# First-pass attention scores issued in twos, one per half of the TensorE array

## The chip, the cores and the metric

The kernel runs on one core of one Trainium2 chip. The metric is the time of one execution on the device in microseconds (us). Three runs of the kernel before gave 1682.65, 1682.81 and 1683.82 us; the median is 1682.81 us.

## The reference

Two blocks follow each other on x of shape (4, 1024, 128), all in float32. Both have 16 heads of width 8.

```python
# block 1
x = x + ln(attn_alibi_causal(ln(x)))     # scores*scale + alibi bias, causal mask, softmax, @v, @Wo
# block 2, on ln(x)
h = h + ln(attention(h)) * g1 + b1       # no mask: every query sees all 1024 keys
h = h + ln(moe(h)) * g2 + b2             # top 2 of 8 experts, gelu(h@W1[e])@W2[e]
x = x + ln(h)
```

Softmax needs the maximum of each row of scores (or a value that plays its part). The kernel finds it in a pass of its own.

## The kernel before, in words

Each attention layer is cut into 16 **slots**: a batch (4) times a group of four heads. Slots 0 to 15 are the causal layer, 16 to 31 the layer without a mask; `SLOTS` is 32. In a slot every head is computed twice.

- **First pass, "a"** (lines 374 to 395): scores with the queries on the 128 partitions of PSUM and up to 512 keys along them; VectorE takes the maximum of each row (`tensor_reduce`, line 589). A head's operands take 32 rows, and one matmul has 64 rows of the array as its contraction (`PAIR`): heads 0 and 1 use the upper half of the array, heads 2 and 3 the lower. Such a matmul is a **chunk**: (query tile, key half, heads, keys). A causal slot has 40 chunks, the other kind 64. They are listed in the head order 0, 2, 1, 3, so neighbours 2k and 2k+1 have the same shape and lie on different halves of the array. When a causal chunk meets the diagonal, two bf16 matmuls (line 393) add the mask into its last 128 keys; 24 of 40 chunks do.
- **Turn, "m" and "mtr"**: when all chunks of a slot are reduced, VectorE combines the maxima (lines 598 to 603), TensorE transposes them (line 399), VectorE copies them out (line 609), and they go into the operands as more rows, so that the second pass yields score minus maximum.
- **Second pass, "b"** (line 411): scores with the keys on the partitions, 512 queries or fewer; ScalarE takes the exponential (line 474) into `probs`. **"pv"** (line 424) multiplies by the values: 4 heads side by side in columns of the array, 8 matmul instructions. Finished outputs are evicted by ScalarE (line 479, "oev").

The work is written out by hand as one list of steps (`program`, lines 174 to 217). Slot s is a loop over its `nq` key tiles (12 when causal, 16 otherwise), called step i here. Step i issues, in this order: the first "b" of tile i+3, half of the step's chunks, the second "b", the other chunks, the third and fourth "b", perhaps "m" or "mtr", then "pv" of tile i+1, and row work such as projections ("turn", "q", "k", "project"). The chunks of a step belong to a later slot: in the first `a_steps` steps to slot s+1 (16 chunks over 5 steps when that is causal, 36 over 9 otherwise), in the last seven to slot s+2 (24 or 28 chunks). They are spread evenly, so that a step has three or four chunks in the causal layer; in the other it has four, except that the turn's step (`mt_step`, the first of the last seven, i = 5 or 9) has three and the step three later has five.

What orders the engines: each engine walks the same list in order and waits on counting semaphores. PSUM has a ring of four banks (`A_BANKS`) for chunks, the turn's transpose and all row matmuls; `bank_free` lets a step have a bank only when the step four places earlier in the ring was read. "b" has three banks, so a "b" waits for the exponential three before it. `probs` has four buffers.

Of the kernel before, what the change touches and what calls it, by code (L numbers as in the profile page):

```python
# [26 lines left out]
P = 128  # L27
# [13 lines left out]
HALF = 512  # L41
# [16 lines left out]
LOADS = 16 * 3 * GH  # L58
# [4 lines left out]
PAIR = 2 * HW  # L63
# [45 lines left out]
def plan_of(s):  # L109
    return PLANS[s // S]  # L110


def place_of(s):

    return s // S, s % S // G, s % G
# [57 lines left out]
def program():  # L173


    rows = row_steps()
    first, second = plan_of(0), plan_of(1)
    out = [("a", 0, c) for c in range(first.na)] + [("m", 0, 0), ("mtr", 0, 0)]
    bs = [("b", 0, i) for i in range(GH * LEAD)]
    ass = [("a", 1, c) for c in range(second.a_next)]  # L180
    for i in range(GH):
        out += ass[len(ass) * i // GH:len(ass) * (i + 1) // GH] + bs[i:i + 1]
    out += [("stage", 0, 0)] + bs[GH:] + [("pv", 0, 0)]
    for s in range(SLOTS):
        p = plan_of(s)
        if s + 3 < SLOTS:
            out.append(("load", s + 3, 0))
        if s + 1 < SLOTS:
            out.append(("stage", s + 1, 0))
        weights = [4 - (i == p.mt_step) - .5 * (i == p.m_step) for i in range(p.nq)]  # L190
        for i in range(p.nq):
            early = i < p.a_steps
            part = range(p.a_steps) if early else range(p.a_steps, p.nq)
            target = s + 1 if early else s + 2
            ass = []
            if target < SLOTS:
                t = plan_of(target)
                base, n = (t.a_next, t.na - t.a_next) if early else (0, t.a_next)
                total = sum(weights[k] for k in part)
                lo = int(n * sum(weights[k] for k in part if k < i) / total + .5)  # L200
                hi = int(n * sum(weights[k] for k in part if k <= i) / total + .5)
                ass = [("a", target, base + c) for c in range(lo, hi)]
            q = i + LEAD
            at, q = (s, q) if q < p.nq else (s + 1, q - p.nq)
            bs = [("b", at, q * GH + j) for j in range(GH)] if at < SLOTS else []
            half = (len(ass) + 1) // 2
            out += bs[:1] + ass[:half] + bs[1:2] + ass[half:] + bs[2:]
            if s + 1 < SLOTS:
                if i == p.m_step:
                    out.append(("m", s + 1, 0))  # L210
                if i == p.mt_step:
                    out.append(("mtr", s + 1, 0))
            at, q = (s, i + 1) if i + 1 < p.nq else (s + 1, 0)
            if at < SLOTS:
                out.append(("pv", at, q))
                if q in plan_of(at).half_end:
                    out.append(("oev", at, plan_of(at).half_end.index(q)))
            out += rows.get((s, i), [])
    return out
# [18 lines left out]
def attend(nc, loaded, query, key, rests, tokens, sums, by_head, dens, inverses, inverse_rows, ident, half_ident,  # L238
           half_mask, km, fq, x_rows, kept_u, wo, bo, wv, bv, wqk, bqk, rows, gate_w, gate_b, gw, tri, rank, table, pows, W1,
           W2, w_parts, routing, xs):  # L240
    steps = program()
    with ExitStack() as ctx:
        def sb(name, shape, dt=F32):
            return ctx.enter_context(nc.sbuf_tensor(f"at_{name}", shape, dt))

        def sem(name):
            return ctx.enter_context(nc.semaphore(f"at_{name}"))
# [26 lines left out]
        raw, parts = sb("raw", [P, FF]), sb("parts", [P, 2, FF], F32R)  # L274

        a_made, a_read = sem("a_made"), sem("a_read")
# [32 lines left out]
        def done(eng, semaphore, kind, s, n, per=1):  # L309

            if (s, n) in number.get(kind, {}):
                eng.wait_ge(semaphore, per * number[kind][s, n])

        def after(eng, name, key):

            r = (name,) + key
            if r in row_number:
                eng.wait_ge(row_done[ENGINE_OF[name]], row_number[r])
# [11 lines left out]
        def query_columns(s, t):  # L330
            qh, kt = plan_of(s).quads[t]
            q0 = max(qh * HALF, kt * P) if plan_of(s).causal else qh * HALF
            return qh, kt, q0, (qh + 1) * HALF - q0

        def bank_of(step):
            return a_bank[place[step] % A_BANKS]
# [13 lines left out]
        def layer(stage):  # L350
            return 0 if stage == "first" else 1
# [4 lines left out]
        def _(pe):  # L356
            def bank_free(step):

                if place[step] < A_BANKS:
                    return  # L360
                what, s, n = ring[place[step] - A_BANKS]
                if what == "a":
                    done(pe, a_read, "a", s, n)
                elif what == "mtr":
                    done(pe, m_read, "mtr", s, n)
                else:
                    reader = dict(project="y", turn="turned", values_mm="values", q="q_out", k="k_out", logits="gate",
                                  rank="pos")[what]
                    after(pe, reader, n)

            for step in steps:
                what, s, n = step
                if what in RING:
                    bank_free(step)
                    misc = bank_of(step)
                if what == "a":
                    l, b, g = place_of(s)
                    qt, kh, heads, w = plan_of(s).chunks[n]

                    if n == 0:  # L380
                        pe.wait_ge(loaded, LOADS * (s + 1))
                    diagonal = plan_of(s).causal and kh * HALF + w == (qt + 1) * P

                    k = len(heads)
                    scores = misc[:, 0:k * w].rearrange("p (k w) -> p k w", k=k)
                    rows_ = slice(PAIR * (heads[0] // 2), PAIR * (heads[0] // 2 + 1))
                    first = heads[0] % 2
                    mm = pe.matmul(scores, fq[g][rows_, qt * P:(qt + 1) * P],  # L388
                                   km[g][rows_, first:first + k, kh * HALF:kh * HALF + w],
                                   start=True, stop=not diagonal)  # L390
                    if diagonal:
                        for i in range(2):
                            mm = pe.matmul(scores[:, :, w - P:w], half_ident[rows_, i, :],  # L393
                                           half_mask[rows_, i, None, :].broadcast_to([PAIR, k, P]),
                                           start=False, stop=(i == 1))
                    mm.then_inc(a_made, 1)
                elif what == "mtr":
                    done(pe, m_split, "m", s, 0)
                    pe.transpose(misc[:, 0:P], m_parts[:, :, :, :].rearrange("p j k t -> p (j k t)").bitcast(F32),
                                 ident[:, :]).then_inc(m_turned, 1)  # L400
                elif what == "b":
                    l, b, g = place_of(s)
                    t, j = n // GH, B_HEADS[n % GH]
                    qh, kt, q0, w = query_columns(s, t)
                    if n == 0:
                        pe.wait_ge(m_landed, MAX_ROWS * (s + 1))
                    k = number["b"][s, n] - 1
                    if k >= B_BANKS:
                        pe.wait_ge(exp_done, k + 1 - B_BANKS)
                    rows_ = slice(PAIR * (j // 2), PAIR * (j // 2 + 1))  # L410
                    pe.matmul(b_bank[k % B_BANKS][:, 0:w], km[g][rows_, j % 2, kt * P:(kt + 1) * P],  # L411
                              fq[g][rows_, q0:q0 + w], start=True, stop=True).then_inc(b_made, 1)
                elif what == "pv":
                    p = plan_of(s)
                    qh, kt, q0, w = query_columns(s, n)
# [7 lines left out]
                    for j in range(GH):  # L423
                        mm = pe.matmul(pv_bank[HW * j:HW * (j + 1), HALF - w:HALF], vst[s % 2][:, kt, j, :],  # L424
                                       probs[n % PROBS][:, j, 0:w], start=(kt == 0), stop=(n == p.half_end[qh]))
                    mm.then_inc(pv_done, 1)
                elif what in ROW_ENGINE["pe"]:
                    stage, k = n
                    i = layer(stage)
                    if what == "project":  # L430
                        after(pe, "heads_t", n)
                        for t in range(HQ):
                            mm = pe.matmul(misc[:, t * P:(t + 1) * P], heads_t[:, t * P:(t + 1) * P],
                                           wo[1 if stage == "enter" else 0][:, :], start=True, stop=True)
                    elif what == "turn":
                        after(pe, "w" if stage == "enter" else "norm2b", n)
                        src = normed[:, :, :] if stage == "first" else block_of(kept_u, k)
                        for t in range(HQ):
                            mm = pe.transpose(misc[:, t * P:(t + 1) * P], src[:, t, :], ident[:, :])
                    elif what == "values_mm":  # L440
                        after(pe, "turned", n)
                        for t in range(HQ):
                            mm = pe.matmul(misc[:, t * P:(t + 1) * P], t32[:, t * P:(t + 1) * P], wv[i][:, :],
                                           start=True, stop=True)
                    elif what in ("q", "k"):
                        after(pe, "low", n)
                        m = "qk".index(what)
                        mm = three(pe, misc[:, :], [part[:, m, :] for part in wqk[i]], [part[:, :] for part in turned])
                    elif what == "logits":
                        after(pe, "low", n)  # L450
                        pe.wait_ge(gw_made, 2)
                        for t in range(HQ):
                            mm = three(pe, misc[:, t * E:(t + 1) * E], [m[:, t * P:(t + 1) * P] for m in turned],
                                       [m[:, :] for m in gw])
                    elif what == "rank":
                        after(pe, "seen", n)
                        pe.matmul(misc[:, 0:TB * E], tri[:, 0, :], routing["either"][:, :, :].rearrange("p t e -> p (t e)"),
                                  start=True, stop=False)
                        mm = pe.matmul(misc[:, 0:TB * E], tri[:, 1, :],
                                       routing["seen"][:, pair_of(k), :].rearrange("p t e -> p (t e)"),  # L460
                                       start=False, stop=True)
# [1419 lines left out]
```

## Time and profile before

| what | value |
|---|---|
| median of three runs | 1682.81 us |
| the profiled execution | 1682.8 us |
| its span, first to last instruction | 1681.1 us |
| TensorE busy | 1424.7 us, 85% |
| VectorE busy | 1296.1 us, 77% |
| ScalarE busy | 1097.2 us, 65% |
| mean granted TensorE clock | 0.915 |

Busy time of TensorE counts matmuls in flight; their ends are modelled, and matmuls on the two halves of the array overlap, so a busy share near one does not say that the array is full. Attention lasts from about 113 us to 1346 us; what follows is the expert layer.

### The profile page before, as it was taken

How to read it: one execution, taken by the hardware profiler on the slowest of the kernel's cores; microseconds unless marked ns; L12 is line 12 of the kernel's file. 1: busy time of each engine (PE TensorE's matmuls, PEld its weight loads, DVE VectorE, ACT ScalarE, POOL GpSimd, SP SyncE). 2: the span in 40 equal slices, each digit the busy share in tenths (PEclk: the TensorE clock that was granted, in tenths of full speed). 3: DMA queues.
4: the chain of work that ended last, by engine and by line, in shares of the span. 5: the costliest groups of instructions: out<-in, count | busy, mean ns of one | idle time of the engine just before them, and what ended most of it. 6: DMA issues, size and time to landing. Idle time of an engine off the chain costs nothing. (4 is left out here: it accounts for less than half of the span.)

```text
span 1681.1 us, 27511 instructions
## 1 busy us (share of the span) xinstructions
PE 1424.7 (85%) x9143; PEld 712.0 (42%) x9143; DVE 1296.1 (77%) x2638; ACT 1097.2 (65%) x2256; POOL 536.7 (32%) x624
## 2 busy tenths in 40 slices
PE   3389999999999999999999999999999831999400
PEld 3145555555555443443344333433343221788300
DVE  4378888889888989999999999999998023655355
ACT  4036677677676557778777787778777820999444
POOL 5114544534525322340122312323141406000274
PEclk9569999999999989999999999999999965999855
DMA  6402241322322222133221122102210124788322
GB/s 168 145 28 73 84 133 50 112 81 65 102 89 72 74 71 66 43 90 91 69 65 53 52 64 78 54 32 75 61 46 33 57 78 131 224 247 248 110 63 69
DMA packets 105822, 148.96 MB, mean 89 GB/s; under 512 B 13236, under 2 KB 63164, under 8 KB 105680
## 3 DMA queue, kind: packets, MB, share of 16 engines
q1 hardware_dynamic: 100348, 138.18, 28.0%
q0 software_dynamic: 4096, 8.40, 1.7%
q8 instruction: 73, 1.20, 0.3%
q10 hardware_dynamic: 1236, 0.62, 0.2%
q14 instruction: 69, 0.57, 0.1%
HBM read 78.70 MB, written 67.13 MB: 87 GB/s over the span
## 5 line engine op out<-in xcount | busy, mean ns | idle before, releaser
L474 ACT ACTIVATE at_probs<-at_b 128x512 f32<-128x512 f32 (+3 forms) x1792 | 866.3, 557 | 380.8 <-PE at_b L411 376.2
L589 DVE TENSOR_REDUCE at_mx<-at_a 128x1 f32<-128x512 f32 (+3 forms) x1664 | 992.0, 661 | 89.5 <-PE at_a L393 28.3
L411 PE MATMUL at_b<-fq,km 64*128 64x512 f32 (+3 forms) x1792 | 669.1, 439 | 16.7 <-ACT at_probs L474 13.3
L388 PE MATMUL at_a<-km,fq 64*128 64x512 f32 (+2 forms) x1664 | 549.9, 453 | 46.3 <-DMA fq<-rest 35.2
L411 PEld LDWEIGHTS at_b<-fq,km 64*128 64x128 f32 x1792 | 295.9, 187 | 405.0 <-ACT at_probs L474 340.5
L424 PE MATMUL at_pv<-at_probs,at_vst 128*32 128x512 f32 (+3 forms) x3584 | 442.0, 566 | 0.0
L388 PEld LDWEIGHTS at_a<-km,fq 64*128 64x128 f32 x1664 | 273.8, 191 | 146.2 <-DVE at_mx L589 82.9
L747 POOL TENSOR_SCALAR_AFFINE_SELECT at_probs<-at_probs 128x512 f32<-128x512 f32 x128 | 81.5, 636 | 284.0 <-ACT at_probs L474 283.1
L1653 POOL DMA_INDIRECT t_got<-expert_out,t_out_pos x64 | 63.5, 993 | 171.4 <-issue 171.4
L424 PEld LDWEIGHTS at_pv<-at_probs,at_vst 128*32 128x32 f32 x3584 | 71.0, 108 | 104.2 <-issue 49.2
L393 PE MATMUL at_a<-half_mask,half_ident 64*128 64x128 bf16 (+1 forms) x768 | 108.7, 251 | 0.0
L1566 DVE TENSOR_TENSOR t_hid_lo<-t_hid,t_hid_hi 128x512 fp32r<-128x512 f32 x92 | 61.3, 686 | 60.5 <-ACT t_hid_hi L1419 60.5
L1414 ACT ACTIVATE t_hid<-t_bank_h,t_bias 128x512 f32<-128x512 f32 x92 | 63.0, 687 | 2.7 <-PE t_bank_h L235 2.6
L752 POOL DMA_INDIRECT expert_rows<-kept_u,route_pos x48 | 46.7, 974 | 36.5 <-DVE route_pos L873 23.5
L1419 ACT ACTIVATE t_hid_hi<-t_hid 128x512 fp32r<-128x512 f32 x92 | 55.5, 635 | 0.0
L393 PEld LDWEIGHTS at_a<-half_mask,half_ident 64*128 64x128 bf16 x768 | 43.2, 100 | 25.6 <-issue 17.4
L1577 DVE SCALAR_TENSOR_TENSOR t_z<-t_got,route_weight,t_weighed 128x128 f32<-128x128 f32 x32 | 9.1, 346 | 47.4 <-ACT t_weighed L1428 47.4
L637 POOL TENSOR_TENSOR at_rstd<-at_mean_var,pow_cols 128x4 f32<-128x4 f32 x26 | 5.3, 203 | 124.9 <-DVE at_mean_var L501 124.9
L479 ACT ACTIVATE at_osb<-at_pv 128x512 f32<-128x512 f32 x64 | 39.4, 615 | 6.2 <-PE at_pv L424 1.9
L741 POOL COPY at_vst<-tokens 128x256 f32<-128x256 f32 x32 | 12.7, 397 | 95.3 <-PE at_pv L424 95.0
L637 POOL TENSOR_TENSOR at_turned_hi<-at_t,pow_cols 128x512 fp32r<-128x512 f32 x18 | 18.7, 1041 | 69.4 <-DVE at_t L532 69.4
L233 PE MATMUL t_bank_h<-t_x_t_hi,t_w 128*128 128x512 f32 x92 | 37.0, 402 | 3.1 <-issue 1.6
(237 smaller groups left out, 1254.2 us busy)
## 6 DMA issues: line engine op xcount, KB each, us to landing
t_w<-w_parts SPq DMA_DIRECT2D x46, 512.0 KB, 4.4
sums<-at_osb SPq DMA_DIRECT2D x64, 256.0 KB, 2.0
fq<-query SPq DMA_DIRECT2D x128, 96.0 KB
km<-key SPq DMA_DIRECT2D x128, 96.0 KB
w_parts<-at_parts SPq DMA_DIRECT2D x16, 512.0 KB, 3.0
query<-at_q_hi SPq DMA_DIRECT2D x24, 256.0 KB, 3.1
key<-at_k_hi SPq DMA_DIRECT2D x24, 256.0 KB, 3.7
t_x_tok<-expert_rows SPq DMA_DIRECT2D x23, 256.0 KB, 4.8
```

The lines of the kernel that those rows point to most:

```text
L388: mm = pe.matmul(scores, fq[g][rows_, qt * P:(qt + 1) * P], km[g][rows_, first:first + k, kh * HALF:kh * HALF + w], start=True, stop=not d ...
L393: mm = pe.matmul(scores[:, :, w - P:w], half_ident[rows_, i, :], half_mask[rows_, i, None, :].broadcast_to([PAIR, k, P]), start=False, sto ...
L411: pe.matmul(b_bank[k % B_BANKS][:, 0:w], km[g][rows_, j % 2, kt * P:(kt + 1) * P], fq[g][rows_, q0:q0 + w], start=True, stop=True).then_in ...
L424: mm = pe.matmul(pv_bank[HW * j:HW * (j + 1), HALF - w:HALF], vst[s % 2][:, kt, j, :], probs[n % PROBS][:, j, 0:w], start=(kt == 0), stop= ...
L474: act.activation(probs[t % PROBS][:, j, 0:w], b_bank[k % B_BANKS][:, 0:w], ACT.Exp).then_inc(exp_done, 1)
L589: dve.tensor_reduce(mx[:, kh, qt, heads[0]:heads[0] + k], bank_of(step)[:, 0:k * w].rearrange("p (k w) -> p k w", k=k), AX.X, ALU.max).the ...
L747: pool.affine_select(block_, block_, [[0, GH], [1, P]], ALU.is_ge, 0.0, base=0, channel_multiplier=-1).then_inc(masked, 1)
L752: pool.indirect_dma_start(out=xs[:, :], out_offset=bass.IndirectOffsetOnAxis(ap=routing["pos"][:, k, t:t + 1], axis=0), in_=kept_u[:, t, : ...
L1414: op = act.activation(hid[:, f, :], h_bank[f][:, :], ACT.Gelu, bias=bias[:, n, f:f + 1])
L1419: op = act.activation(hid_hi[i][:, f, :], hid[:, f, :], ACT.Identity)
L1566: op = dve.tensor_tensor(hid_lo[i][:, f, :], hid[:, f, :], hid_hi[i][:, f, :].bitcast(F32), ALU.subtract)
L1653: pool.indirect_dma_start(out=got[i][:, k, t, :], out_offset=None, in_=ys[:, :], in_offset=bass.IndirectOffsetOnAxis(ap=out_pos[:, k, n * ...
```

## The change

Three things change, in `program` and in TensorE's walk.

1. The boundaries of the chunks of a step are rounded to even numbers, and so is the place where the step's chunks are split around its second "b". Every step has 2, 4, 6 or 8 chunks, always whole pairs.
2. TensorE takes a pair at a time: the bank and the score of the first chunk, the bank and the score of the second, then mask matmul 1 of both, then mask matmul 2 of both (before: score, mask 1, mask 2 of one chunk, then the same of the next).
3. Nothing changes for the other engines but the order of the list.

```diff
-                lo = int(n * sum(weights[k] for k in part if k < i) / total + .5)
-                hi = int(n * sum(weights[k] for k in part if k <= i) / total + .5)
+                lo = 2 * int(n * sum(weights[k] for k in part if k < i) / total / 2 + .5)
+                hi = 2 * int(n * sum(weights[k] for k in part if k <= i) / total / 2 + .5)
...
-            half = (len(ass) + 1) // 2
+            half = 2 * ((len(ass) + 2) // 4)
...
+            def first_scores(pair):
+                parts = []
+                for step in pair:
+                    what, s, n = step
+                    bank_free(step)
+                    l, b, g = place_of(s)
+                    if n == 0:
+                        pe.wait_ge(loaded, LOADS * (s + 1))
+                    qt, kh, heads, w = plan_of(s).chunks[n]
...
+                    mm = pe.matmul(scores, fq[g][rows_, qt * P:(qt + 1) * P],
+                                   km[g][rows_, heads[0] % 2:heads[0] % 2 + k, kh * HALF:kh * HALF + w],
+                                   start=True, stop=not diagonal)
+                    if diagonal:
+                        parts.append((rows_, k, scores[:, :, w - P:w]))
+                    else:
+                        mm.then_inc(a_made, 1)
+                for i in range(2):
+                    for rows_, k, corner in parts:
+                        mm = pe.matmul(corner, half_ident[rows_, i, :],
+                                       half_mask[rows_, i, None, :].broadcast_to([PAIR, k, P]),
+                                       start=False, stop=(i == 1))
+                        if i == 1:
+                            mm.then_inc(a_made, 1)
+
+            for at_, step in enumerate(steps):
                 what, s, n = step
+                if what == "a":
+                    if n % 2 == 0:
+                        assert steps[at_ + 1] == ("a", s, n + 1)
+                        first_scores(steps[at_:at_ + 2])
+                    continue
```

By the formula, a causal slot's steps i = 0 to 11 had 3, 4, 3, 3, 3, 3, 3, 4, 3, 4, 3, 4 chunks and get 4, 2, 4, 4, 2, 2, 4, 4, 4, 2, 4, 4. In a slot of the second layer steps 9 to 15 had 3, 4, 4, 5, 4, 4, 4 and get four each; steps 0 to 8 have four before and after.

## Rows read from the trace of the kernel before

**Rows 1.** Stretches: start:end, PE, PEld, DVE, ACT, POOL busy us, clock, DMA share, GB/s
```profile
113.00:571.80 458.80, 453.66 (x3678) 235.12 (x3677) 398.73 (x829) 320.68 (x750) 205.85 (x261) 1.00 0.28 84
619.90:1314.40 694.50, 676.40 (x4036) 275.26 (x4035) 636.93 (x1167) 516.98 (x995) 177.35 (x199) 0.99 0.21 63
571.80:619.90 48.10, 45.85 (x228) 20.32 (x227) 43.43 (x80) 23.02 (x51) 14.66 (x18) 0.86 0.11 30
```
**Rows 2.** Waits of the weight loads: us in total, times, longest us
```profile
PEld at_b L411 <- ACT at_probs L474: 340.5, 552, 1.7
PEld at_a L388 <- DVE at_mx L589: 82.9, 295, 1.9
```
**Rows 3.** Timeline (start us, us, engine, operation), a step of slot 24
```profile
1002.38 0.50 PE L411 MATMUL at_b<-fq,km 64*128 64x512 f32 x1
...
1002.91 2.06 ACT L474 ACTIVATE at_probs<-at_b 128x512 f32<-128x512 f32 x4 [0.54 <-PE at_b L411]
...
1003.56 0.18 PEld L411 LDWEIGHTS at_b<-fq,km 64*128 64x128 f32 x1 [0.29 <-ACT at_probs L474]
...
1004.98 0.50 PE L411 MATMUL at_b<-fq,km 64*128 64x512 f32 x1
```
**Rows 4.** Timeline, ScalarE, slot 31, whose steps have no chunks
```profile
1323.74 2.07 ACT L474 ACTIVATE at_probs<-at_b 128x512 f32<-128x512 f32 x4 [0.53 <-PE at_b L411]
1326.34 2.07 ACT L474 ACTIVATE at_probs<-at_b 128x512 f32<-128x512 f32 x4 [0.53 <-PE at_b L411]
```
**Rows 5.** Timeline, TensorE, slot 8, step 8, chunks 10 to 12
```profile
380.15 0.33 PE L411 MATMUL at_b<-fq,km 64*128 64x128 f32 x1
380.16 0.59 PE L388 MATMUL at_a<-km,fq 64*128 64x512 f32 x2
380.51 0.28 PE L393 MATMUL at_a<-half_mask,half_ident 64*128 64x128 bf16 x2
380.60 0.30 PE L411 MATMUL at_b<-fq,km 64*128 64x128 f32 x1
380.61 0.28 PE L393 MATMUL at_a<-half_mask,half_ident 64*128 64x128 bf16 x2
...
381.16 0.53 PE L424 MATMUL at_pv<-at_probs,at_vst 128*32 128x384 f32 x4
```
**Rows 6.** Timeline, VectorE, reduces of slot 8's steps 7 and 8 from chunk 6
```profile
378.66 3.55 DVE L589 TENSOR_REDUCE at_mx<-at_a 128x1 f32<-128x384 f32 x6 [0.71 <-PE at_a L393]
```
**Rows 7.** Timeline, slots 8 and 9: reduces from chunk 20, then step 0 on TensorE
```profile
359.25 4.38 DVE L589 TENSOR_REDUCE at_mx<-at_a 128x1 f32<-128x512 f32 x7 [0.16 <-PE at_a L388]
...
361.10 0.33 PE L411 MATMUL at_b<-fq,km 64*128 64x128 f32 x1
...
362.05 0.53 PE L424 MATMUL at_pv<-at_probs,at_vst 128*32 128x384 f32 x4
```
**Rows 8.** Timeline, TensorE, step 9 of slot 8: four chunks
```profile
381.94 0.50 PE L411 MATMUL at_b<-fq,km 64*128 64x512 f32 x1
...
383.24 0.48 PE L411 MATMUL at_b<-fq,km 64*128 64x512 f32 x1
```
**Rows 9.** Timeline, the turn's step of slot 19
```profile
787.13 0.50 PE L411 MATMUL at_b<-fq,km 64*128 64x512 f32 x1
...
788.39 1.87 DVE L589 TENSOR_REDUCE at_mx<-at_a 128x1 f32<-128x512 f32 x3
788.73 0.14 PEld L399 LDWEIGHTS at_a<-ident,at_m_parts 128*128 128x128 f32 x1 [0.24 <-issue]
```
**Rows 10.** Stretches that are steps 8, 9 (turn), 10 and 12 (five chunks) of slot 21
```profile
877.95:880.56 2.61, 2.61 (x17) 1.01 (x16) 2.50 (x5) 2.06 (x4) 0.00 (x0) 1.00 0.00 0
880.57:883.43 2.86, 2.86 (x20) 1.15 (x16) 2.72 (x14) 2.06 (x4) 0.06 (x1) 1.00 0.00 0
883.44:886.76 3.32, 3.12 (x20) 1.18 (x16) 3.32 (x7) 2.08 (x4) 2.60 (x4) 1.00 0.01 2
...
889.38:892.34 2.96, 2.66 (x21) 1.10 (x17) 2.86 (x5) 2.17 (x4) 1.05 (x1) 1.00 0.00 0
```
**Rows 11.** Timeline, the turn's step of slot 21
```profile
882.18 0.14 PEld L399 LDWEIGHTS at_a<-ident,at_m_parts 128*128 128x128 f32 x1 [0.25 <-issue]
...
883.01 1.85 DVE L589 TENSOR_REDUCE at_mx<-at_a 128x1 f32<-128x512 f32 x3
```
**Rows 12.** Slot 20's turn: TensorE, and the stretch behind it
```profile
833.42 0.45 PE L399 MATMUL at_a<-ident,at_m_parts 128*128 128x128 f32 x1 [1.81 <-DVE at_m_parts L603]
833.80 1.93 PE L424 MATMUL at_pv<-at_probs,at_vst 128*32 128x512 f32 x8
...
837.57 1.06 PE L424 MATMUL at_pv<-at_probs,at_vst 128*32 128x512 f32 x8
```

More of the change, by code:

```diff
@@ L369, in bank_free @@
                     after(pe, reader, n)
-            for step in steps:
-                what, s, n = step
+            def first_scores(pair):
[7 more added lines that the diff above has]
+                    qt, kh, heads, w = plan_of(s).chunks[n]
+                    k = len(heads)
+                    scores = bank_of(step)[:, 0:k * w].rearrange("p (k w) -> p k w", k=k)
+                    rows_ = slice(PAIR * (heads[0] // 2), PAIR * (heads[0] // 2 + 1))
+                    diagonal = plan_of(s).causal and kh * HALF + w == (qt + 1) * P
+                    mm = pe.matmul(scores, fq[g][rows_, qt * P:(qt + 1) * P],
[13 more added lines that the diff above has]
+            for at_, step in enumerate(steps):
+                what, s, n = step
+                if what == "a":
[3 more added lines that the diff above has]
+                    continue
                 if what in RING:
@@ L375, in _ @@
                     misc = bank_of(step)
[L376 to L397, printed above, removed]
+                if what == "mtr":
                     done(pe, m_split, "m", s, 0)
```

## The prediction

> **What bounds the kernel now.** I read four views, in this order. The table by stretch comes first [rows 1]: the causal layer (113 to 572 us) and the unmasked one (620 to 1314 us) make up two thirds of the span. In both TensorE is busy 97 to 99% by the profile and VectorE 87 to 92%. Two engines near full can't both be the bound, so the rest is reading which wait ends last in a step.
>
> The waits say it [rows 2]: the second pass's weight loads wait 340.5 us for ScalarE's exponentials, the first pass's 82.9 us for VectorE's reduces. The timeline of a plain step shows how [rows 3]. A "b" starts at 1002.38, its exponential at 1002.91 (0.53 later) and takes about 0.6; then the step's fourth "b" may load its weights, at 1003.56; "pv" comes 0.43 behind, and the next first "b" at 1004.98. That loop, "b", exponential, fourth "b", "pv", is 2.60 us long. The proof that chunks hide in it is slot 31, which has none: its exponentials also come 1326.34 - 1323.74 = 2.60 us apart [rows 4]. So a step costs the loop, and a chunk costs something only where it makes the third or fourth "b", the turn or "pv" later than the loop would. In the causal layer the loop is shorter where "b" or "pv" is narrow, so there the cover is thinner.
>
> **The change part by part.**
>
> *Mask order.* It removes no instruction: 768 mask matmuls before and after. What it could gain is overlap of the halves. The diagonal step shows that the halves already run past each other [rows 5]: the list says b, score, mask, mask, score, mask, mask, b, and yet both scores start before the first mask (380.16, two in 0.59 us), and the second "b" (380.60) starts before the last two masks (380.61). A half's own sequence is the same before and after, so I take 0. The upper end of a gain is that the second score of a diagonal pair lost one score and two masks, about 0.23 + 0.13 us by the starts in these rows; the lower end is a loss where the second chunk's bank comes late, since the masks of the first now stand behind that wait: one reduce, 0.6 us, but then VectorE has older chunks to work on. Value 0.
>
> Here the Trainium skill differs. "TensorE: Matmul & The Clock Gate", section "Part 3: Packing small matmuls", says that matmuls start and end strictly in program order and only weight loads are pulled ahead. By that rule the old order would have held the second score behind the first one's masks, and the new order would free it; the trace does not agree, since the starts just read cross program order. What the rule would make of the time is the first rival below.
>
> *Causal layer, uneven steps.* Two steps that had three narrow-loop chunks get four.
> - Step 0. The new fourth chunk needs the bank of chunk 23. Seven reduces start at 359.25, about 0.6 us apart [rows 7]; the fourth, chunk 23's, ends near 361.73, which is 0.63 after step 0's first "b" (361.10). Then load and score, 0.1 + 0.23, the fourth "b" and "pv": about 1.17 after the first "b", where "pv" stood at 0.95 (362.05). Cost 0.22. In 12 of 15 slots; in three a projection stands ahead and the bank is free. 2.6 us.
> - Step 8. The new chunk 13 needs chunk 9's bank. Six reduces from 378.66 last 3.55 in all [rows 6], so the fourth (chunk 9) ends near 380.9, 0.73 after the first "b". By the same sum "pv" comes 1.26 after it instead of 1.01 (381.16 - 380.15) [rows 5]. Cost 0.25, in the 11 slots without row work right there: 2.8 us.
> - Steps 9 and 1 had four chunks and get two. The last "b" stood 1.30 behind the first (383.24 - 381.94) [rows 8], against 1.18 in the loop [rows 3]. A gain of 0.09 and 0.05, in 15 slots: -2.1 us.
> - A norm's statistics stall step 2 in six slots by some 0.4 us; fewer chunks queue behind them: about -0.1 each, -0.6 us (an estimate from the reduce's 0.6 us spacing).
> Sum +2.7 us. Its ends: -3, if the fourth chunks cost nothing and the stalls go, and +8, if each costs one reduce more.
>
> *Unmasked layer, the turn's step.* It gets a fourth chunk, and that moves the ring. The transpose used to take the bank of the previous step's last chunk, long read. Now it takes the bank of this step's first chunk, whose reduce stands behind VectorE's chain for the turn. In a quiet slot that reduce starts at 788.39 and ends 0.68 later, 789.07, while the transpose loaded its weights at 788.73 [rows 9]: 0.38 late, and "pv" with it. In slot 21 VectorE does a norm's statistics between: the reduces start at 883.01, the first ends near 883.67, the transpose stood at 882.18 [rows 11]: 1.5 late. There are three such slots (21, 25, 29; by the same reading 1.5 to 1.8).
>
> *The step of five.* It goes: 2.96 against 2.61 us [rows 10], -0.36. In slot 21 step 10 was also stretched, 3.32 against 2.61 [rows 10], since its chunks waited for the late reduces; when "pv" is 1.5 later this wait lies beside it: -0.7.
>
> By kind of slot: three like 21 cost 1.5 (1.8 once) - 0.7 (1.0 once) - 0.36, so +0.43 each, +1.3. Quiet ones +0.38 - 0.36 = 0 (four). Four with a projection, as slot 20: there the chain for the turn ended at 833.2 and the first reduce behind it ends at 833.9, so +0.5; their five-chunk step with a projection loses 0.5; 0. In slots 22 and 26 VectorE works without a pause through these steps, so the count of reduces decides and that is the same: 0. Slots 14, 15 and 17 shift a reduce into a step with room, -0.6 in all. Sum +0.7.
>
> *The clock.* In slot 20 TensorE stood idle 1.81 us before the transpose, and "pv" then took 1.93 us instead of 1.06: the granted clock was at the lower of its levels (1.2 GHz) behind it. From "pv" to "pv" took 3.77 instead of 2.60 us [rows 12], so a fall costs 1.2 us. It follows such an idle in four of four slots. The three slots like 21 will now stand idle some 1.7 to 2 us. I count one and a half falls, +1.8; ends 0 and 3 x 1.2 = 3.6 (and 4 x 1.2 more if the falls of the four project slots get a second stretch).
>
> **Sum.** 2.7 + 0.7 + 1.8 = +5.2 us on the profiled execution's 1682.8 us (span 1681.1 and 1.7 around it), which is the median of the runs shown. Forecast 1688.0 us.
>
> **Rivals.**
> *A, matmuls in program order.* Then the mask order gains. For: the profile models the ends of matmuls. Against: the starts of [rows 5]. It would decide only where a half's queue sets "pv": two diagonal steps of a causal slot (7 and 8; elsewhere the exponential is later), some 0.25 us of the 0.36 each, in 16 slots: -8. Time 1680. (The rule of the skill named above is this one.) Chance 0.12.
> *B, the stalls and slow-clock stretches at the layers' seam go.* Slots 14 and 15 have to make 28 + 36 chunks of the wide kind; in 571.8 to 619.9 us VectorE is busy 43.4 of 48.1 us and the granted clock is 0.86 [rows 1]. If whole pairs keep TensorE fed so that four slow stretches there and one in slot 22 don't occur, 5 x 1.2 = 6 us come off, and about 2 more if the turn's step is less delayed: 1688 - 8 = 1680. It decides when TensorE's idle between reduces shortens. Against: that stretch is set by VectorE's reduces, whose number is the same. On the other side of no change. Chance 0.15.
> *C, the fourth chunks cost nothing.* If a chunk overlaps with its half's "b" more than I allow, the causal sum is about 0 and falls of the clock stay one: 1684.5. Chance 0.18.
> *D, more falls.* All seven lengthened idles bring a slow stretch, 7 x 1.2 in place of 1.8, and the steps at the seam with eight chunks add to it: 1695. Chance 0.1.
>
> **How the numbers follow.** The forecast has the rest, 0.45, its own range 1685.5 to 1691. A measurement tells 0.2%, 3.4 us, from no change: 1679.4 and 1686.2. Faster gets half of A and two thirds of B, 0.16. Same gets the other parts of A and B (0.11), most of C (0.16) and 0.04 of the forecast, 0.31. Slower is what is left, 0.53. The range 1679 to 1696 takes in A, B and D; the bounds of the causal sum (-3 to +8) lie within it.
>
> **What the changed profile would show.** The turn's transpose (line 399) with waits for VectorE in nearly all slots from 16 on, up to 1.5 us in slots 21, 25 and 29; no step of 2.96 us, steps of four chunks at 2.60 unchanged; causal steps 0 and 8 longer by 0.2 us, 1 and 9 shorter by less than 0.1; mask matmuls with the same starts relative to their half; a clock below 1.00 near slots 21, 25 and 29. I am wrong if the transpose starts as early as before, if diagonal steps get shorter by 0.2 us, or if the seam (slots 14 and 15) changes by more than 2 us.

## The result, and the profile after

The change made the kernel slower: 1697.41 us (median of 4 runs, 1693.94 to 1697.74) against 1683.32 us (4 runs, 1682.65 to 1684.06). The ratio is 1.0084, 95% interval [1.0071, 1.0097], so some 14 us where 5 had been forecast. The profiled execution took 1697.7 us (span 1696.0); in it TensorE was busy 1429.0 us, VectorE 1297.7 and ScalarE 1097.1, as before within 0.3%, at a mean granted clock of 0.912. The work is the same; the waits are not. Below are the stretches of the kernel after (columns as in [rows 1]): the causal slots 0 to 14, the seam (slot 15), and slots 16 to 31.

```profile
112.48:581.55 469.07, 459.97 (x3678) 234.88 (x3677) 399.27 (x829) 323.23 (x750) 205.83 (x261) 0.99 0.28 82
581.55:632.20 50.65, 48.41 (x229) 21.39 (x228) 43.61 (x79) 23.25 (x51) 14.65 (x18) 0.76 0.10 28
632.20:1365.14 732.94, 702.77 (x4208) 281.82 (x4211) 638.03 (x1167) 542.81 (x1049) 192.94 (x215) 0.99 0.21 63
```
[Rows 1] has the causal slots and the seam of the kernel before, 458.8 and 48.1 us; its unmasked row stops earlier, so here is the whole of slots 16 to 31 of the kernel before:

```profile
619.92:1350.05 730.13, 706.05 (x4208) 284.04 (x4211) 636.91 (x1167) 545.31 (x1049) 193.21 (x215) 0.99 0.21 63
```
So +10.2 us in the causal slots, +2.6 at the seam, +2.8 in the unmasked layer. The causal part is the surprise. The waits of the weight loads (columns as in [rows 2]) both grew: behind ScalarE from 340.5 us and 552 times, behind VectorE from 82.9 us and 295 times.

```profile
PEld at_b L424 <- ACT at_probs L487: 357.4, 599, 1.6
PEld at_a L385 <- DVE at_mx L602: 90.9, 350, 1.9
```
To see where, take the distance from the start of one "pv" to the start of the next as the length of a step. Slot 8 has no row matmul; its slot time went from 27.39 to 28.12 us, as in slots 4 and 12. The step lengths in us, for both kernels and for two experiments told below (chunks in brackets where they differ):

| step | before | after | fours_0_8 | fours_6_10 |
|---|---|---|---|---|
| 11 of slot 7 | 1.86 | 2.24 | 1.86 | 2.22 |
| 0 | 1.94 (3) | 2.09 (4) | 2.17 (4) | 1.94 (3) |
| 1 | 2.42 (4) | 2.40 (2) | 2.40 (3) | 2.39 (3) |
| 6 | 2.38 (3) | 2.38 (4) | 2.38 (3) | 2.38 (4) |
| 7 | 2.21 | 2.56 | 2.21 | 2.56 |
| 8 | 2.01 (3) | 2.01 (4) | 2.27 (4) | 2.00 (3) |
| 9 | 2.48 (4) | 2.39 (2) | 2.39 (3) | 2.39 (3) |
| 10 | 2.00 (3) | 1.96 (4) | 1.96 (3) | 1.95 (4) |

The loss is in steps 7 and 11, which have four chunks in every column. Step 7 of the kernel before, TensorE from its first "b" to "pv", then VectorE:

```profile
377.94 0.38 PE L411 MATMUL at_b<-fq,km 64*128 64x256 f32 x1
...
378.44 0.49 PE L388 MATMUL at_a<-km,fq 64*128 64x512 f32 x2
378.76 0.29 PE L393 MATMUL at_a<-half_mask,half_ident 64*128 64x128 bf16 x4
378.85 0.37 PE L411 MATMUL at_b<-fq,km 64*128 64x256 f32 x2
379.15 0.64 PE L424 MATMUL at_pv<-at_probs,at_vst 128*32 128x512 f32 x4
...
376.33 1.62 DVE L589 TENSOR_REDUCE at_mx<-at_a 128x2 f32<-128x512 f32 x3 [0.75 <-PE at_a L393]
378.66 1.02 DVE L589 TENSOR_REDUCE at_mx<-at_a 128x1 f32<-128x384 f32 x2 [0.71 <-PE at_a L393]
```
The same step of the kernel after, TensorE with its weight loads, then VectorE:

```profile
384.49 0.38 PE L424 MATMUL at_b<-fq,km 64*128 64x256 f32 x1
...
385.32 0.18 PEld L385 LDWEIGHTS at_a<-km,fq 64*128 64x128 f32 x1 [0.17 <-DVE at_mx L602]
...
385.42 0.36 PE L424 MATMUL at_b<-fq,km 64*128 64x256 f32 x1
385.67 0.28 PE L394 MATMUL at_a<-half_mask,half_ident 64*128 64x128 bf16 x2
385.76 0.36 PE L424 MATMUL at_b<-fq,km 64*128 64x256 f32 x1
386.05 0.64 PE L437 MATMUL at_pv<-at_probs,at_vst 128*32 128x512 f32 x4
...
383.05 3.78 DVE L602 TENSOR_REDUCE at_mx<-at_a 128x2 f32<-128x512 f32 x7 [1.55 <-PE at_a L394]
```
Before, step 6 leaves three reduces. They end at 376.33 + 1.62 = 377.95, just as step 7 starts, and VectorE then stands idle 0.71 us: each bank that step 7 wants is free. After, step 6 leaves four; VectorE works on without a pause, and the fourth reduce (chunk 5's) ends near 383.05 + 4 x 0.54 = 385.2, 0.7 after the step's first "b" (384.49). The ring has four banks, so the fourth chunk of step 7 (chunk 9) takes chunk 5's: it loads at 385.32, released by VectorE. Its masks and the last "b" stand behind it. That "b" comes 1.27 after the first, where before the last two "b" came 0.91 after the first, and "pv" with it: +0.35. Step 11 does the same behind step 10 (chunk 23 takes chunk 19's bank), with two such waits in the rows of the kernel after:

```profile
393.26 0.18 PEld L385 LDWEIGHTS at_a<-km,fq 64*128 64x128 f32 x1 [0.20 <-DVE at_mx L602]
393.86 0.18 PEld L385 LDWEIGHTS at_a<-km,fq 64*128 64x128 f32 x1 [0.41 <-DVE at_mx L602]
...
392.20 3.40 DVE L602 TENSOR_REDUCE at_mx<-at_a 128x2 f32<-128x256 f32 x6
```
The second kind of loss is in steps with a row matmul and a new fourth chunk. In slots 1 to 3 the step with "q" went from 2.90 to 3.29 us. A row matmul takes a ring bank too, and the step's new fourth chunk is four places behind it. In the row of slot 1 after, that chunk waits for VectorE to evict "q", and two "b" wait with it, where in before the same two "b" loaded 0.63 after the step's first one:

```profile
170.03 0.18 PEld L424 LDWEIGHTS at_b<-fq,km 64*128 64x128 f32 x1 [0.36 <-issue]
...
170.95 0.18 PEld L385 LDWEIGHTS at_a<-km,fq 64*128 64x128 f32 x1 [0.20 <-DVE at_q_out L557]
170.95 0.29 PEld L424 LDWEIGHTS at_b<-fq,km 64*128 64x128 f32 x2
```
The step with "project" in slots 5, 9 and 13 went from 3.06 to 3.42 in the same way: in slot 5 the fourth chunk waits 0.45 us for VectorE to evict the projection. The step with the values' matmul in slots 0 to 3 went from 3.47 to 3.66, and in slots 7 and 11 two steps with a row matmul grew by 0.40 and 0.25; what holds these is not shown. There are gains too: the stall behind the norm's statistics fell from 2.57 to 2.43 in slots 1 to 3 and to 2.27 in slots 5, 9 and 13, step 9 by 0.09 in most slots, and step 1 by 0.2 to 0.3 in slots 6, 7, 10, 11 and 14.

A part of the causal loss is the clock's. Step 1 of slot 0, of the kernel before and of the kernel after:

```profile
116.33:118.73 2.40, 2.40 (x24) 1.28 (x23) 2.37 (x9) 1.53 (x5) 0.64 (x1) 1.00 0.00 0
115.83:119.17 3.34, 3.34 (x20) 1.69 (x19) 3.31 (x13) 1.50 (x4) 0.63 (x1) 0.61 0.00 0
```
The +0.95 stands beside a clock of 0.61 in place of 1.00. Two of the experiments told below agree: the same step takes 3.34 at a clock of 0.67 in short_before, which has the old numbers of chunks, and 2.54 in even_only, which has the new ones.

Added up over slots 0 to 14, steps 7 and 11 cost 7.3 us, the steps with a row matmul 4.7, step 0 elsewhere 1.9 and this stretch 0.95; all other steps together give back 4.6. By slot: +1.6 in slot 0, +2.9 in slots 1 to 3, +2.2 in 4, 8, 12, +0.8 in 5, 9, 13, +1.1 in 6 and 10, +1.7 in 7 and 11, -0.1 in 14; together +10.2.

The seam grew in steps 0 to 4 of slot 15, which have six to eight chunks: from 28.13 us at a mean clock of 0.76 to 30.85 at 0.61. Behind them, at full clock in both kernels, its turn's step went from 2.86 to 3.28 and its former five-chunk step from 2.93 to 2.33.

In the unmasked layer the turn's step of slot 19, then that of slot 21 and its former five-chunk step, of the kernel after:

```profile
798.47:801.71 3.24, 2.93 (x19) 1.15 (x18) 3.14 (x8) 2.70 (x7) 0.00 (x0) 1.00 0.00 0
...
892.91:897.32 4.41, 2.93 (x19) 1.15 (x18) 4.27 (x16) 3.05 (x7) 0.54 (x2) 1.00 0.00 0
902.53:905.14 2.61, 2.61 (x18) 1.01 (x17) 2.49 (x5) 2.07 (x6) 1.21 (x1) 1.00 0.00 1
```
They were 2.86, 2.86 and 2.96 us ([rows 10] for slot 21). The transpose waits for the step's own first chunk, in slot 21 behind VectorE's statistics; rows of slot 19 and of slot 21 after:

```profile
801.45 0.14 PEld L412 LDWEIGHTS at_a<-ident,at_m_parts 128*128 128x128 f32 x1 [0.62 <-DVE at_mx L602]
...
895.15 0.86 DVE L511 BATCH_NORM_STATS2 at_stats<-at_y 128x6 f32<-128x128 f32 x4
...
896.35 1.25 DVE L602 TENSOR_REDUCE at_mx<-at_a 128x1 f32<-128x512 f32 x2
897.06 0.14 PEld L412 LDWEIGHTS at_a<-ident,at_m_parts 128*128 128x128 f32 x1 [1.79 <-DVE at_mx L602]
```

### The profile page after: what moved, and what is told of

It is laid out like the page before. It is cut to its first block and busy times, and to the rows that moved or that the text cites. A ratio compares the mean times of both kernels' runs of the same rounds, so it can differ in the third digit from the quotient of the medians.

```text
span 1696.0 us, 27511 instructions
## 1 busy us (share of the span) xinstructions
PE 1429.0 (84%) x9143; PEld 709.2 (42%) x9143; DVE 1297.7 (77%) x2638; ACT 1097.1 (65%) x2256; POOL 537.4 (32%) x624
## 5 line engine op out<-in xcount | busy, mean ns | idle before, releaser
L424 PE MATMUL at_b<-fq,km 64*128 64x512 f32 (+3 forms) x1792 | 682.9, 438 | 18.4 <-ACT at_probs L487 10.8
L424 PEld LDWEIGHTS at_b<-fq,km 64*128 64x128 f32 x1792 | 304.4, 188 | 418.0 <-ACT at_probs L487 357.4
```

## Experiments

In all of them "slots 0 to 14" is the stretch from the first "pv" of slot 0 to that of slot 15, 458.9 us in the kernel before and 469.1 after.

**even_only: even numbers, old mask order.**

```diff
-                        first_scores(steps[at_:at_ + 2])
+                        first_scores([step])
```


> Even numbers of chunks per step, but each chunk with its own two masks behind it, as before. Theory 1 (VectorE's reduces run late behind steps of four, so the fourth chunk waits for its bank and holds back the last b of the next step): within 2 us of the changed kernel, 1695 to 1699, and causal steps 0, 7 and 11 as long as there (2.22 us for the one that ends at pv 0, 2.55 at pv 8). Rival 2 (the interleaved masks cost the 0.35 us, since both long steps, 7 and 11, are steps with masks): these steps fall back to 1.86 and 2.21, and the time to about 1688.

Measured 1693.66 us, ratio 1.0072 [1.0051, 1.0093]; slots 0 to 14 took 468.5 us. Its step 7 of slot 8:

```profile
382.77:385.32 2.55, 2.55 (x27) 1.33 (x25) 2.55 (x6) 1.76 (x6) 0.63 (x1) 1.00 0.12 35
```
The loss is there without the new mask order, and so is the long step 7. The time came out just under the 1695 to 1699 expected and 3.7 us below the kernel after. That is not the mask order at work on the causal steps: slots 1 to 14 take as long in both within 0.1 us, and the difference lies where the clock was low in one of them, in slot 0 (-0.6), at the seam (49.1 us at a clock of 0.83) and in the unmasked layer (730.3 us).

**masks_only: old numbers, masks of both chunks interleaved where a pair stands together.**

```diff
-                lo = 2 * int(n * sum(weights[k] for k in part if k < i) / total / 2 + .5)
+                lo = int(n * sum(weights[k] for k in part if k < i) / total + .5)
...
+                    if n % 2 == 0 and steps[at_ + 1] == ("a", s, n + 1):
+                        pair, taken = steps[at_:at_ + 2], {at_ + 1}
```


> The numbers of chunks of before; where the two chunks of a pair follow each other in the list, scores first and then the masks in turn. Theory 1: no change, within 1 us of the kernel before (about 1683.3), steps 7 and 11 at 2.21 and 1.86. Rival 2: steps 7 and 11, where both pairs are adjacent, become 0.3 longer, 15 slots x 0.65 = +10 us. A kernel whose matmuls ran in program order would get faster by some us.

Measured 1683.42 us, ratio 1.0003 [0.9993, 1.0013]; slots 0 to 14: 458.7 us, every step of slot 8 as before within 0.01. TensorE in its step 7:

```profile
377.36 0.38 PE L429 MATMUL at_b<-fq,km 64*128 64x256 f32 x1
...
377.86 0.48 PE L386 MATMUL at_a<-km,fq 64*128 64x512 f32 x2
378.18 0.29 PE L395 MATMUL at_a<-half_mask,half_ident 64*128 64x128 bf16 x4
378.27 0.36 PE L429 MATMUL at_b<-fq,km 64*128 64x256 f32 x2
```
The starts after the first "b" (0.50, 0.82, 0.91) are those of before (0.50, 0.82, 0.91). The mask order is worth nothing measurable.

**even_causal and even_plain: the new numbers for the chunks of one layer, new mask order in both.**

```diff
+                unit = 2 if target < S else 1      # even_plain: target >= S
+                lo = unit * int(n * sum(weights[k] for k in part if k < i) / total / unit + .5)
```


> The change for chunks of causal slots only; chunks of slots 16 to 31 keep the old numbers. Theory 1: +10 us over before (slots 0 to 14), slot 15 and the second layer as before: 1693. If the late layer change is what matters: 1684.

> The change for chunks of slots 16 to 31 only. Theory 1: steps of slots 0 to 13 as before, the turn's step 3.25 instead of 2.86 and the step of five 2.60 instead of 2.97 in quiet slots, sum zero; +2.5 in slot 15 and +3 in the second layer with its slow clock stretches: 1686 to 1689.

Measured: even_causal 1692.95 us, 1.0058 [1.004, 1.0076]; even_plain 1686.2 us, 1.0024 [1.0011, 1.0036]. About +10 and +4 us: the two parts add up to the whole, and the larger is the causal layer's. Slots 0 to 14 took 468.8 and 459.4 us. The seam did not follow the expectation: even_causal was to leave it as before, and it took 49.7 us at a clock of 0.73; in even_plain it took 50.4 at 0.76.

**short_before and short_after: VectorE's reduces in the causal layer over half their columns.** Both leave out the other half of each maximum there.

```diff
-                                      bank_of(step)[:, 0:k * w].rearrange("p (k w) -> p k w", k=k),
+                                      bank_of(step)[:, 0:k * w].rearrange("p (k w) -> p k w", k=k)[:, :, 0:w // (2 if s < S else 1)],
```


> The kernel before with one thing left out: in the causal layer (slots 0 to 15) VectorE takes the maximum over the first half of a chunk's columns only, so a reduce lasts about 0.34 instead of 0.60 us. Control for the next run. Theory 1: slots 0 to 14 lose only what little hung on reduces, some 0.3 us in a quiet slot (27.4 to about 27.0) and the stalls behind statistics; slot 15, which is bound by reduces, gets far shorter.

> The same cut of the causal reduces in the changed kernel. Theory 1 (late reduces hold the banks): steps 0, 7 and 11 fall back to the lengths of the control (about 1.94, 2.21 and 1.86), and slots 0 to 14 take as long as in the control within 2 us. Rival (a half of the array has too much in one step of four chunks, whatever VectorE does): the three steps stay 0.16, 0.34 and 0.36 us longer than in the control, +10 us in slots 0 to 14.

Measured 1666.24 and 1673.42 us (ratios to the kernel before 0.9902 [0.9879, 0.9926] and 0.9947 [0.993, 0.9965]). Slots 0 to 14: 452.8 and 456.6. The difference of the two rules fell from 10.2 to 3.9 us. Step 1 of slot 0, with its slow clock, is long in the kernel after (3.34) but here in short_before (3.34 against 2.50 in short_after); without that step the difference fell from 9.3 to 4.7. In slot 8 steps 0, 7 and 11 are 1.94, 2.21 and 1.90 us in short_after, against 1.94, 2.21 and 1.86 in short_before. VectorE in step 7 of short_after:

```profile
366.89 1.28 DVE L602 TENSOR_REDUCE at_mx<-at_a 128x2 f32<-128x256 f32 x4 [1.55 <-PE at_a L394]
369.05 0.95 DVE L602 TENSOR_REDUCE at_mx<-at_a 128x1 f32<-128x192 f32 x3 [0.88 <-PE at_a L394]
```
The same four reduces of step 6 now end at 368.17, before step 7 starts (368.33), and the pause is back. So it is the late reduces that make steps 7 and 11 long, not the number of chunks. What stays is the row work: "q" 3.29 against 2.90, "project" 3.46 against 3.07, the step with the values 3.66 against 3.47. My expectation that slot 15 would get far shorter in short_before missed: it took 49.9 us. The chunks worked on there belong to slots 16 and 17, whose reduces are whole in both kernels.

**turn_later: the kernel after, with the transpose of the unmasked slots one step later.**

```diff
-                if i == p.mt_step:
+                if i == p.mt_step + (s >= S):
```


> The changed kernel with the turn's transpose of slots 17 to 31 issued at the end of the step after (step 10 instead of 9). Its bank is then that of step 10's first chunk. If the wait for the reduce behind VectorE's chain is what made the turn's step 3.25, the two steps together fall from 5.85 to about 5.65 (quiet slot), since the reduces are only 0.6 late by then and the transpose waits 0.2; in slots 21, 25 and 29 from 7.0 to 6.0 and without slow clock stretches. Time 1692, 5 below the changed kernel. If the wait is for something else (the chain itself or a DMA), no change.

Measured 1694.57 us, 1.0071 [1.005, 1.0092] to the kernel before; 1692 had been expected. The two steps concerned in slot 19, and the second of them in slot 21:

```profile
795.62:798.22 2.60, 2.60 (x18) 1.01 (x17) 2.50 (x7) 2.07 (x6) 0.00 (x0) 1.00 0.00 0
798.22:801.32 3.10, 3.00 (x18) 1.07 (x17) 3.10 (x6) 2.43 (x6) 0.00 (x0) 1.00 0.00 0
892.37:896.63 4.26, 4.00 (x18) 1.43 (x18) 4.23 (x13) 2.54 (x6) 2.34 (x4) 1.00 0.00 0
```
In slot 19 3.24 + 2.60 became 2.60 + 3.10, and in slot 21 the delay moved one step on (4.41 to 4.26). My expectation that a later turn would take most of it away there failed: the delay is VectorE's queue, and whoever stands behind it pays.

**fours_0_8 and fours_6_10: the old numbers but for which steps of a causal slot have four chunks.** The list gives chunks of steps 0 to 4 and 5 to 11 (before: 3, 4, 3, 3, 3 and 3, 3, 4, 3, 4, 3, 4).

```diff
+COUNTS = {(True, True, True): (4, 3, 3, 3, 3), (True, True, False): (3, 3, 4, 4, 3, 3, 4)}   # fours_0_8
+COUNTS = {(True, True, True): (3, 3, 4, 4, 2), (True, True, False): (2, 4, 4, 3, 3, 4, 4)}   # fours_6_10
...
+                    lo, hi = sum(own[:at_]), sum(own[:at_ + 1])
```


> The kernel before with four chunks in steps 0 and 8 of a causal slot (early counts 4,3,3,3,3, late 3,3,4,4,3,3,4), so those are the only steps of the causal layer with one more chunk, and steps 7 and 11 find the statistics of three-chunk steps before them. The prediction's own term (fourth chunk costs what its score chain costs): step 0 of a quiet slot 1.94 to 2.16 us, step 8 2.01 to 2.26, slots 0 to 14 +2 to +3 us. Theory of the bank (a fourth chunk pays where the bank that it writes is still being read): steps 7 and 11 stay at 2.21 and 1.86; the q step of slots 0 to 3 goes from 2.90 to 3.29 and the project step of slots 5, 9, 13 from 3.06 to 3.42, because the fourth chunk takes the bank of the row matmul; quiet step 8 gains nothing or under 0.1. Slots 0 to 14: +3 to +4.5 us, median +2 to +4. Rival (the loss sits in the number of chunks per step as such): the same +0.35 in steps 0 and 8 here.

> The kernel before with four chunks in steps 6, 7, 10 and 11 (early counts 3,3,4,4,2, late 2,4,4,3,3,4,4), steps 0 and 8 as before or shorter. Theory of the bank: four chunks in steps 6 and 10 make their statistics end late, and the fourth chunk of steps 7 and 11 waits for the banks: step 7 of a quiet slot 2.21 to 2.55, step 11 1.86 to 2.22; the q step and the project step keep 2.90 and 3.06. Slots 0 to 14: +4 to +6 us, median +4 to +6. The prediction's own term (score chains of steps 0 and 8 alone): steps 7 and 11 unchanged, slots 0 to 14 within 1 us of before.

Measured: fours_0_8 1685.16 us, 1.0021 [1.0011, 1.0031]; fours_6_10 1687.69 us, 1.0041 [1.0027, 1.0056]. Slots 0 to 14 took 462.5 and 465.0 us, +3.7 and +6.1, together 9.8 of the 10.2. That they add up so nearly is partly chance: 0.95 of fours_0_8 is the slow step 1 of slot 0 (3.35 us at a clock of 0.64), both kernels have the gain of step 9, and the cost of step 8 goes when they are combined. The steps are in the table above. Step 8 of slot 8 in fours_0_8, then steps 7 and 8 in fours_6_10:

```profile
381.40:383.66 2.26, 2.26 (x22) 1.10 (x20) 2.21 (x5) 1.22 (x4) 0.64 (x1) 1.00 0.15 34
```
```profile
380.00:382.56 2.56, 2.56 (x26) 1.34 (x25) 2.56 (x6) 1.76 (x6) 0.63 (x1) 1.00 0.12 35
382.56:384.56 2.00, 2.00 (x20) 0.97 (x19) 1.61 (x4) 1.05 (x4) 0.64 (x1) 1.00 0.33 86
```
fours_0_8 is the prediction's causal sum made into a kernel: step 0 +0.23 and step 8 +0.25, as worked out, and "q" 3.29, "project" 3.45, which had been left out. There the theory of the bank as I then held it missed: it allowed step 8 under 0.1. Here the fourth chunk costs what its own chain costs; in the kernel after it costs nothing (2.01), because step 7 before it is already 0.35 late: the bank's last reader, chunk 9's reduce, ends 0.38 after the first "b" of step 8 there and 0.73 after it in fours_0_8. fours_6_10 has the rest: steps 7 and 11 at 2.56 and 2.22, "q" and "project" untouched at 2.90 and 3.03.

**tuned_causal and tuned_both: an attempt to do better.** Four chunks were put where the profile of before has room; tuned_both also has four in each of the last seven steps of an unmasked slot, and the later turn.

```diff
+COUNTS = {(True, True, True): (3, 3, 3, 4, 3), (True, True, False): (4, 3, 4, 3, 3, 3, 4)}
+# tuned_both also: (False, False, False): (4, 4, 4, 4, 4, 4, 4), and the edit of turn_later
```


> The kernel before, with other numbers of chunks in causal slots: 3, 3, 3, 4, 3 in steps 0 to 4 and 4, 3, 4, 3, 3, 3, 4 in steps 5 to 11, masks as before. By theory 1 a fourth chunk is free where the step has cover: in the turn's step (its chunks are the smallest) and in step 3 (the output's eviction holds it anyway), and step 9 and 1 lose theirs: -0.09 in a quiet slot, -0.2 behind q and k. Together 2 to 3 us: 1680.5. If reduces don't matter here, no change.

> As tuned_causal, and four chunks in each of the last seven steps of the second layer's slots with the transpose of the turn one step later: another 0.36 - 0.2 us in 14 slots, -2 us, in all 1678.5. If the later turn delays the next slot's first b (its rows come by DMA), steps 13 get longer and the time rises.

Measured 1681.91 us, 0.9998 [0.999, 1.0007], and 1682.11 us, 1.0004 [0.9995, 1.0012]. In tuned_causal slots 0 to 14 gained 1.3 us (457.5) of the 2 to 3 expected: step 9 lost its 0.09, but the stall behind the statistics moved one step on (step 3 went from 2.48 to 2.77) and the turn's step of slots 4, 8 and 12 went from 2.86 to 3.08. In tuned_both they gained 0.4 (458.4), and its time is 3.6 us above the 1678.5 expected. Neither beats the kernel before.

**before_again and after_again: both kernels unchanged, once more.**

> The kernel before, unchanged, profiled a second time on another visit to a chip. If the length of the seam (slot 15) goes by the slow-clock stretches that happen to fall there: 48 to 50 us, with a granted clock between 0.86 and 0.73 that need not be the 0.86 of the first profile. If the seam's 48.1 us belongs to this kernel's chunk numbers: 48.1 +- 0.2 at 0.86 again. Slots 0 to 14: 458.9 +- 0.3 either way.

> The changed kernel, unchanged, profiled a second time. Seam by the clock alone: 48 to 50.7 us, following the granted clock as in the other kernels. Seam by the even numbers: 50.6 +- 0.2 again. Slots 0 to 14: 469.1 +- 0.3 either way.

One run each, 1679.0 and 1702.1 us. The stretches of before_again, then those of after_again:

```profile
112.47:571.23 458.76, 453.59 (x3678) 235.19 (x3677) 398.90 (x829) 320.51 (x750) 205.46 (x261) 1.00 0.28 84
571.23:619.29 48.06, 45.74 (x228) 20.28 (x227) 43.39 (x79) 23.08 (x51) 14.64 (x18) 0.86 0.11 30
619.29:1346.18 726.89, 703.65 (x4209) 283.10 (x4212) 635.98 (x1167) 544.98 (x1049) 192.94 (x215) 0.99 0.21 63
```
```profile
112.71:581.77 469.06, 460.03 (x3678) 234.62 (x3677) 399.07 (x829) 323.14 (x750) 205.84 (x261) 0.99 0.27 82
581.77:632.52 50.75, 48.33 (x228) 21.42 (x227) 43.58 (x79) 23.25 (x51) 14.66 (x18) 0.76 0.10 28
632.52:1370.38 737.86, 707.82 (x4208) 282.77 (x4211) 637.56 (x1167) 543.06 (x1049) 192.98 (x215) 0.98 0.21 62
```
The causal slots repeat within 0.1 us. So does the seam, clock included: the idea that its slow stretches fall differently from one execution to the next fell. The unmasked layer does not repeat: 726.9 and 730.1 us for one kernel, 732.9 and 737.9 for the other. Over all profiles slots 16 to 31 took 726.9 to 730.9 us in the eight kernels or repeats with the old list there and 730.3 to 737.9 in the five with the list of the kernel after.

The seam's length goes mostly with its clock across the kernels, and not with the chunk numbers alone: masks_only, with the old numbers, has 49.0 us at a clock of 0.79; even_only, with the new ones, 49.1 at 0.83; and short_before, with the old numbers and the old mask order, this:

```profile
553.43:603.30 49.87, 49.00 (x228) 21.95 (x227) 43.65 (x79) 23.13 (x51) 14.66 (x18) 0.73 0.09 29
```
The numbers have a share as well: at the same clock of 0.83 the seam took 49.1 us in even_only and 48.2 in tuned_causal, whose numbers there are the old ones, so some 0.9 us of the 2.6 may be theirs. What sets the clock there stays open.

## Why the prediction was wrong

*What bounds the kernel* was right: a step costs the loop, and a chunk costs where it makes the last "b" or "pv" later. short_before bears it out: a third less work for VectorE in the causal slots bought 6 of 459 us.

*Mask order, 0:* right (1.0003), and rival A with its rule of program order fell: in the record the two halves already overlapped, and the new order changed no start.

*Causal layer, +2.7:* this step failed; it was +10.2, of which 0.95 is a slow clock in slot 0 that no term had. Four terms of it:
- "Two steps that had three narrow-loop chunks get four." I priced only the steps in which a narrow loop meets its own fourth chunk. Steps 6 and 10 also get four, and that was taken as covered by their own loop. It is (2.38 as before, and 1.96 against 2.00), but their fourth reduce ends 0.7 into the next step, whose fourth chunk wants that bank. fours_6_10 shows it at +0.35 in step 7 and +0.36 in step 11, and short_after shows that it goes when the reduces are short. The +6.1 us of fours_6_10 is some +7.4 in these two steps, less what other steps gained.
- "In three a projection stands ahead and the bank is free": it isn't. The row matmul's bank is the one the fourth chunk takes, and the step with "project" costs +0.36; "q" in slots 0 to 3 (+0.39) and the other row matmuls with a new fourth chunk had no term at all. Together they are 4.7 us, and they are most of what short_after leaves.
- Step 0 +0.22 and step 8 +0.25 were right for a kernel that changes these alone (fours_0_8: +0.23, +0.25). In the real change they are +0.15 and 0, since the steps before are already late. Steps 9 and 1 of a quiet slot: -0.09 as said, and -0.02 where -0.05 was said.
- The gains were larger than the 2.7 us put down for them, 4.6: step 1 fell by 0.2 to 0.3 in five slots, and the stall behind the statistics gave 1.3 in its six slots, not 0.6. This hid a part of the missing costs.

The upper end given for this sum, +8, was also too low: it counted a reduce for each of the two steps, not for their neighbours.

*Unmasked layer, +0.7:* right but for one part. The turn's step of the quiet slots +0.38 (predicted +0.38), of slot 21 +1.55 (+1.5); the five-chunk step 2.96 to 2.60; step 10 of slot 21 3.32 to 2.61; slots 21 and 25 +0.47 and +0.44 (+0.43 predicted), quiet ones 0.0. The part that failed is the -0.6 for slots 14, 15 and 17: slot 14 gave -0.05, slot 17 +0.03, and in slot 15 the shorter step 8 stood beside a longer turn's step.

*Clock, +1.8:* near in the unmasked layer of the first profile, too low for the whole kernel. In the unmasked layer it is a fall in slot 29 and a second slow stretch in slot 20, less one that the kernel before had in slot 22, together +1.1 us (by the slots' times, less slot 29's own 0.45). The 0.95 of slot 0 and the larger part of the seam's 2.6 come on top, and they had been put at nothing. In slot 20 of the kernel after, TensorE idles 2.18 before the transpose, and two "pv" in a row are slow, where [rows 12] has one:

```profile
846.12 0.47 PE L412 MATMUL at_a<-ident,at_m_parts 128*128 128x128 f32 x1 [2.18 <-DVE at_mx L602]
846.53 1.94 PE L437 MATMUL at_pv<-at_probs,at_vst 128*32 128x512 f32 x8
...
850.59 1.90 PE L437 MATMUL at_pv<-at_probs,at_vst 128*32 128x512 f32 x8
852.43 0.50 PE L424 MATMUL at_b<-fq,km 64*128 64x512 f32 x1
```
In after_again slots 21, 24, 25 and 26 are slower by 1.2 to 2.5 us more, so rival D has some truth in some executions.

*Seam:* forecast unchanged, with more than 2 us named as a sign of error; it is +2.6. Rival B expected a gain there and got the opposite, a clock of 0.76 in place of 0.86. Rival C (fourth chunks cost nothing) fell.

By stretch: causal 7.5 us missed (0.95 of it the clock's), seam 2.6, the rest within 1 us. That last is in part luck, since the unmasked layer alone moves by up to 5 us between two executions.

## What to carry to other kernels

When work is redistributed between steps around a ring of buffers, price the step *behind* each one that gets more, not only the one that gets it: walk the ring place by place, and for each use find who read that buffer last and when that read now ends. Every user of the ring counts, row matmuls and transposes too. Rounding a spread to even numbers turned a pattern of 3 and 4 into one of 2 and 4, and fours behind each other or behind a row matmul, not the pairs, made most of the loss.

## What was not expected of the hardware

- Delays in neighbouring steps are not additive: +0.25 us in step 8 vanished behind +0.35 in step 7, and two half-changes of +0.36 and +0.56 us in a quiet slot gave 0.72 together.
- The granted clock at the seam repeats for a kernel (0.86 twice, 0.76 twice), while edits to the causal slots ahead of it moved it between 0.86 and 0.73. In the unmasked layer it wanders from one execution to the next by up to 5 us of the kernel's time.
